# A two-layer transformer on one core: three places in a hand-written step order, and other buffer places

## What is computed

```python
x = _layernorm(x + _L0_attn_ref(x, ...))   # 16 heads of 16, relu weights, causal
x = _layernorm(x + _L0_ffn_ref(x, ...))    # Hadamard-rotated weights, 256 -> 1024 -> 256
x = _layernorm(x + _L1_attn_ref(x, ...))   # 32 query heads, 8 key/value heads of 64, window of 64, RoPE, softmax
x = _layernorm(x + _L1_ffn_ref(x, ...))    # silu(gate) * up, down, 256 -> 1024 -> 256

def _layernorm(x, axis=-1, eps=1e-05):
    m = jnp.mean(x, axis=axis, keepdims=True)
    v = jnp.var(x, axis=axis, keepdims=True)
    return (x - m) / jnp.sqrt(v + eps)

# second feed-forward
gate = jnp.einsum('bsd,hd->bsh', x, w_gate)
up = jnp.einsum('bsd,hd->bsh', x, w_up)
gated = jax.nn.silu(gate) * up
return jnp.einsum('bsh,dh->bsd', gated, w_down)
```

## Time and profile before

| | us |
|---|---|
| median of 3 runs | 527.74 (526.45 to 528.85) |
| the profiled execution | 527.04 |
| its span, first to last instruction | 524.4 |
| PE busy | 472.9 (90%) |
| DVE busy | 385.0 (73%) |
| ACT busy | 335.9 (64%) |
| POOL busy | 236.1 (45%) |

### The profile page before, as it was taken

The page is one execution under the profiler, slowest core; times in us unless marked ns, Lnnn a source line. Parts: engine busy times, 40 slices in busy tenths (PEclk is TensorE's granted clock), DMA queues, the critical chain, the costliest instruction groups (busy, mean ns, idle before and its releaser), DMA issues.

```text
span 524.4 us, 10779 instructions
## 1 busy us (share of the span) xinstructions
PE 472.9 (90%) x3848; PEld 400.3 (76%) x3848; DVE 385.0 (73%) x675; ACT 335.9 (64%) x940; POOL 236.1 (45%) x167
## 2 busy tenths in 40 slices
PE   2899997999999975999999999988996988899994
PEld 2454654788889964899999999978896877788884
DVE  4455597778562689998898998889889974543534
ACT  3555555634643439888888989859888798332230
POOL 0377537221640756655566566545656523400001
PEclk9999998999999997999999999989999899999998
DMA  8500010033310000000000000001001222000101
GB/s 272 176 16 2 2 41 0 1 120 92 97 66 20 1 1 0 23 20 3 22 23 21 21 23 21 8 15 40 24 12 50 62 62 81 1 0 1 41 0 40
DMA packets 8611, 19.96 MB, mean 38 GB/s; under 512 B 1392, under 2 KB 2928, under 8 KB 8432
## 3 DMA queue, kind: packets, MB, share of 16 engines
q1 hardware_dynamic: 8560, 19.29, 11.9%
HBM read 18.23 MB, written 1.05 MB: 37 GB/s over the span
## 4 chain that ended last, share of the span: by engine, by line
PE 72%; DVE 11%; ACT 8%; issue 5%; POOL 1%; DMA 1%; DVEq 0%; POOLq 0%; ACTq 0%; SPq 0%
PE psum L383 16%; PE psum L385 15%; PE psum L384 15%; PE psum L614 5%; PE psum L430 4%; PE psum L602 4%; PE psum L592 4%; ACT probs L846 4%; PE psum L448 4%; PE psum L573 2%; DVE minus_max L1122 1%; PE psum L582 1%; DVE rope_cos_part L1078 1%; DMA raw_chunks<-in_w 1%; DVE out_t_low L897 1%
## 5 line engine op out<-in xcount | busy, mean ns | idle before, releaser
L846 ACT ACTIVATE probs<-psum,minus_max 128x128 f32<-128x128 f32 x256 | 92.6, 398 | 18.7 <-PE psum L592 10.4
L1240 POOL TENSOR_TENSOR rope_sin_part<-qkv_rows,sin_weighted 128x640 f32<-128x640 f32 x32 | 49.1, 1556 | 62.3 <-DVE rope_cos_part L1091 39.5
L1249 POOL TENSOR_TENSOR rms_inverse<-rms_inverse,minus_half 128x20 f32<-128x20 f32 x16 | 64.0, 3999 | 1.3
L846 ACT ACTIVATION_READ_ACCUMULATOR probs<-psum,minus_max 128x1 f32 x256 | 60.4, 236 | 0.0
L818 ACT CAST hidden_high<-hidden 128x512 fp32r<-128x512 f32 x32 | 19.8, 620 | 62.4 <-DVE hidden L1037 62.4
L1122 DVE TENSOR_REDUCE minus_max<-psum 128x4 f32<-128x512 f32 x64 | 42.4, 684 | 15.7 <-PE psum L592 14.3
L383 PE MATMUL psum<-x_t_high,ug_high 128*128 128x512 f32 x128 | 51.2, 400 | 0.0
L385 PE MATMUL psum<-x_t_high,ug_low 128*128 128x512 f32 x128 | 50.7, 396 | 0.0
L384 PE MATMUL psum<-x_t_low,ug_high 128*128 128x512 f32 x128 | 50.4, 394 | 0.0
L1116 DVE TENSOR_TENSOR probs<-probs,prob_inverse 128x512 f32<-128x512 f32 x64 | 47.6, 744 | 2.2
L383 PE MATMUL psum<-qkv_high,x_t_high 128*128 128x384 f32 x128 | 46.3, 362 | 0.0
(11 more groups left out here) (146 smaller groups left out, 1403.4 us busy)
## 6 DMA issues: line engine op xcount, KB each, us to landing
raw_chunks<-in_ug SPq DMA_DIRECT2D x8, 512.0 KB, 3.9
raw_chunks<-in_wout SPq DMA_DIRECT2D x16, 256.0 KB, 2.8
raw_chunks<-in_qkv SPq DMA_DIRECT2D x8, 384.0 KB, 3.3
raw_chunks<-in_x SPq DMA_DIRECT2D x2, 512.0 KB, 4.5
raw_chunks<-in_w SPq DMA_DIRECT2D x2, 512.0 KB, 6.4
down_tree<-in_down SPq DMA_DIRECT2D x1, 1024.0 KB, 8.4
x_rows<-in_x_rows SPq DMA_DIRECT2D x2, 512.0 KB, 4.8
raw_chunks<-in_down SPq DMA_DIRECT2D x2, 512.0 KB, 3.4
```

Source lines behind the costliest of these rows:

```text
L846: e = nc.scalar.activation(pr[:, c, q, :], o[:, q * P:(q + 1) * P], ACT.Exp, bias=negm[:, c, q:q + 1], accum_out=psum1[:, c, q:q + 1])
L1240: last = nc.gpsimd.tensor_tensor(ov[:, :, :, z, :], rv[:, :, :, 1 - z, :], sv[:, :, :, z, :], ALU.mult)
L1249: nc.gpsimd.tensor_tensor(r, r, half[:], ALU.pow).then_inc(rr_done, 1)
```

## The change

Every step of a feed-forward is cut in two, `up(layer, n)` and `down(layer, n, *halves)`, and the layer norm in `ln_add`, `ln_stats`, `ln_norm` and POOL's `ln_half`. `later_steps` is replaced by tables for each engine: `..._FILL` (from the feed-forward's tile 10 to the seventh pass), passes 7 to 12 by the old pass tables, `..._DRAIN` (the rest of the passes and the first 8 tiles of the second feed-forward), and a short list for the end. Within a pass nothing is put in another order. What each engine does is otherwise in the old order, with these exceptions:

1. In the fill, DVE does `ln(1, 1)` before `values1(1)`, `rope_sums(0)`, `square_sums(1)`, `normed(0)` and `cosines(1)`, not after them; POOL's part stands before `sines(1)`. `xt(2, 1)` comes earlier: on PE after the first q transpose of iteration 0 rather than of iteration 1, on ACT before `squares(2)`, on DVE right after `cosines(1)`.
2. At the start of the second feed-forward PE does `up 1 3` before `down 1 0`, `down 1 1` and `xt(3, 1)`; DVE does `up 1 2` before `ln(2, 1)`, and `up 1 3` before its part of `xt(3, 1)`; ACT does `up 1 3` before its part.
3. In the last tiles the downs follow three ups behind, and the downs 13, 14 and 15 of the last batch run first for the first half of its rows and then for the second. DVE's additions and statistics follow each half, as before.
4. The weight pieces of the second feed-forward are split in the order ug 0, ug 1, down 0, ug 2, ug 3, down 1 (before: four ug, two down).

The buffers lie elsewhere: the weights of both feed-forwards and `qkv` with high and low side by side for each piece, `wout_low` behind `k_t`, and six slots instead of three for the hidden tiles of the second feed-forward. The waits follow the new neighbours. An extract:

```diff
-FLAG = 2
+HIDDEN_SLOTS = [3, 6]
-FFN1_CHUNKS = [("ug1", c) for c in range(4)] + [("down1", c) for c in range(2)]
+FFN1_CHUNKS = [("ug1", 0), ("ug1", 1), ("down1", 0), ("ug1", 2), ("ug1", 3), ("down1", 1)]
...
+VECTOR_FILL = [("up", 0, 10), ("up", 0, 11), ("xt", 2, 0), ("up", 0, 12), ("up", 0, 13), ("up", 0, 14), ("up", 0, 15),
+    ("values1", 0), ("square_sums", 0), ("cosines", 0), ("ln_add", 1, 1, 0), ("ln_stats", 1, 1, 0),
+    ("ln_add", 1, 1, 1), ("ln_stats", 1, 1, 1), ("ln_norm", 1, 1, 0), ("ln_norm", 1, 1, 1), ("values1", 1),
...
+def last_steps():
+    s = []
+    for n in range(8, B * NI):
+        s.append(("up", 1, n))
+        if n != 12:
+            s.append(("down", 1, n - 2 if n < 12 else n - 3))
+        if n == NI + 1:
             s.append(("ln", 3, 0))
-    s.append(("ln_last",))
+    for half_ in range(2):
+        s += [("down", 1, n, half_) for n in range(B * NI - 3, B * NI)]
+        s += [("ln_add", 3, 1, half_), ("ln_stats", 3, 1, half_), ("ln_half", half_)]
+    s += [("ln_norm", 3, 1, half_) for half_ in range(2)]
...
             qn = place(s, "roped", [TT, GN], F32)
+            qt1 = place(s, "q_t", [2, NQ, 2, WIN], F32)
+            place(s, "until_down0", [512])
+            kt1 = place(s, "k_t", [2, T], F32)
             wol = place(s, "wout_low", [2, 2, C], F32R)
-            qt1 = place(s, "q_t", [2, NQ, 2, WIN], F32)
-            kt1 = place(s, "k_t", [2, T], F32)
             pr = place(s, "probs", [4, 4, P], F32)
...
+            def down(layer, n, *halves):
...
+                for t in [2 * half_ + t2 for half_ in halves or range(2) for t2 in range(2)]:
...
             def up(layer, n):
+                if layer and n == 0:
+                    for read in (ss_done, cos_done, sin_done, v1_done, rope_sum):
+                        act.wait_ge(read, NIT)
...
             def turn1k(k):
+                if k == 0:
+                    filled(act, ("ffn", 0, NI + 6, 1))
...
             def exps(k, c):
                 if k:
                     filled(act, ("turn1p", k - 1, c))
+                else:
+                    filled(act, ("ffn", 0, B * NI - 1, 0))
...
             def normed(k):
                 if k == 0:
-                    filled(dve, ("y", 1, B - 1, 1))
+                    filled(dve, ("ffn", 0, NI + 3, 0))
```

More of the change, by code:

```diff
@@ new lines @@
+GPSIMD_DRAIN = [("sines", 11), ("wout", 8), ("rms_inverses", 11), ("ln", 2, 0), ("sines", 12), ("wout", 9),
+    ("rms_inverses", 12), ("sines", 13), ("wout", 10), ("rms_inverses", 13), ("sines", 14), ("wout", 11),
+    ("rms_inverses", 14), ("chunk", ("ug1", 0)), ("sines", 15), ("wout", 12), ("rms_inverses", 15),
+    ("chunk", ("ug1", 1)), ("wout", 13), ("chunk", ("down1", 0)), ("wout", 14), ("chunk", ("ug1", 2)), ("wout", 15),
+    ("chunk", ("ug1", 3)), ("chunk", ("down1", 1)), ("ln", 2, 1)]
@@ L360, in post_ln_two_layers, with up_weights, down_weights @@
         hi_no = {}
+        def up_weights(layer, c, z):
+            return ug0[c // 2][:, z, c % 2, :] if layer == 0 else w1["ug1", c][:, z, :]
+        def down_weights(layer, c, z):
+            return dn0[c][:, z, :] if layer == 0 else w1["down1", c][:, z, :]
         block = ctx.enter_context(nc.Block())
@@ L387, in _, with first @@
             acc = {}
+            begun = set()
+            def first(step, k):
+                new = (step, k) not in begun
+                begun.add((step, k))
+                return new
             def x_ready(layer, b):
@@ new lines, in up @@
+            def up(layer, n):
+                b, i = divmod(n, NI)
+                if i == 0:
+                    x_ready(1 + 2 * layer, b)
+                if layer == 0:
+                    emptied(pe, *[("prep_ug", i // 2, m) for m in range(KB)])
+                else:
+                    chunk_wait(pe, ("ug1", i // 2))
+                wh, wl = [up_weights(layer, i // 2, z) for z in range(2)]
+                for u in (1, 0):
+                    o, done = claim(("ffn", layer, n, u))
+                    for kb in range(KB):
+                        at = kb * 512 + (i % 2) * 256 + u * P
+                        mm = three(o, (wh[:, at:at + P], wl[:, at:at + P]), (xh[:, b, kb, :], xl[:, b, kb, :]),
+                                   kb == 0, kb == KB - 1)
+                    mm.then_inc(done, 1)
@@ L685, in chunk_target @@
                 return [a[:, c % 2].rearrange("p k t -> p (k t)") for a in (woh, wol)]
-            return [a[:, c, :] for a in {"qkv": (qkvh, qkvl), "ug1": (ug1h, ug1l), "down1": (dn1h, dn1l)}[name]]
+            return [(qkv[:, c] if name == "qkv" else w1[name, c])[:, z, :] for z in range(2)]
         @block.sync
```

309 lines of the change are left out of this document (169 added, 140 removed), and 42 rows, old and new, of tables (SCALAR_DRAIN, SCALAR_FILL, SCALAR_FIRST, TENSOR_DRAIN).

## The result

The changed kernel took 531.30 us, the median of 4 runs (530.36 to 532.65); the kernel before, beside it on the same chip, 527.10 (526.25 to 528.85, 4 runs). The ratio is 1.0074, with a 95% interval of 1.0042 to 1.0106: slower by about 4 us. The forecast was 532.5, with a range of 528.6 to 535.2. The profiled execution took 531.57 with a span of 529.9, against 527.04 and 524.4: 5.5 us longer.

The account below looks back on a forecast made before the run. PE was taken to bound the attention passes, DVE the fill (182 to 212 us). Fill 2.7, second feed-forward 1.4 plus clock 1.7, end -1.0 made +4.8: 532.5 us, own range 530.5 to 534.5, 8 in 10 528.6 to 535.2.

Parts of the forecast that it names:

- What costs nothing: Whole kernel: buffer places, added waits, chunk order and cut steps cost nothing; `normed(0)`'s dropped wait frees nothing.
- Place 1, the mechanism: Fill, 178 to 212 us: early `ln(1,1)` waits 1.97, starts 180.28; `normed(0)` ends 193.5; PE waits 8.4, then about 1.5.
- Place 1, the term: Fill: `maxima(1,0)` starts at 214.7 against 212.01, +2.7 that stays; bounds +0.65 and +4.45.
- so `scores1(0,0)` is done about 201.3: Fill: after half-clock PE work and ACT's copies ending about 200.1, scores end about 201.3 and `maxima(0,0)` starts at 201.35.
- The payback: Fill, after `normed(1)`: early `xt(2,1)` saves DVE 1.28, its wait falls from 0.72 to about 0.25; +4.45 becomes +2.7.
- In the fill I expect one such stretch again, so nothing is added there: Fill: one half-clock stretch as before, so no clock cost is added to the forecast there.
- Place 2, the idle: Second feed-forward's start: `ln(2,1)` starts at 456.87, 5.66 later; PE arrives 4.24 later; idle 1.32 becomes 2.74, +1.4.
- Place 2, the clock: Second feed-forward's start: the 2.74 idle drops the clock to half for some 3.4 us, +1.7.
- The rival with full clock there, 530.8: Second feed-forward's start: clock holds, as an idle between 2.31 and 2.53 or below decides; 530.8, chance 0.20.
- Place 3: Kernel's end: last three downs by halves; DVE's second addition starts 0.32 after PE's last matmul starts, 517.10 for 518.06, -1.0.
- The sum: Whole kernel: 2.7 + 1.4 + 1.7 - 1.0 = +4.8 on a span of 524.4, 532.5; chance 0.48.
- The shared pair: Fill: by the skill's GpSimd/VectorE rule `cosines(1)` waits for the POOL power and ends 3.6 later; +0.8, 533.3, chance 0.03.

Follow-up runs that it names:

- best_fill_free: Changed kernel with the fill's old order and DVE's `ln(2,1)` again before `up 1 2`, plus 24 unread matmuls into a free bank in PE's 6.08 us wait: 525.54 us, 0.9959.
- stall_filled: Changed kernel plus 32 unread 512-column matmuls in PE's list ahead of its wait for `normed(0)` (8.58 us): ratio 1.0036 to the kernel before.

## Why the prediction was right, and where not

- **What costs nothing**: right. With the three places undone the ratio was 0.9991 (0.9977 to 1.0005).
- **Place 1, the mechanism**: right, step by step. `ln(1,1)` started at 180.28 + 0.77, to the hundredth (after 1.90 of idle, 1.97 forecast), and `normed(0)` ended at 194.50 where I had 193.5 + 0.77. The waits of 8.58 and 0.95 answer to the forecast 8.4 and 1.5.
- **Place 1, the term**: mis-sized, 4.3 in this trace (3.6 to 3.8 in others with the same fill) for my 2.7; 1.84 of it is there without the half clock. Of the 1.6 that are missing, 0.2 is `normed(0)`. The step that failed is "so `scores1(0,0)` is done about 201.3": by the trace it took 9.04 from `roped` to the first maxima, and I had 7.85 (1.2). I had let the half clock last about as long as behind the 6.09, some 3.4 us, and it lasted 5.7. By the four traces with this fill (8.32 with 4.1 us of it, 9.04 with 5.7) that is most of the difference. From there to `normed(1)`'s end it took 4.42 where I had 4.95 (-0.5), for the sine products no longer ran beside that step. The payback was 1.1 and not 1.75 (+0.7): DVE's wait ahead of `maxima(1,0)` grew to 0.85, where I had let it shrink to 0.25. "In the fill I expect one such stretch again, so nothing is added there" was the thought behind it, and it is wrong. The stretch moved from a place where it is free, behind the 6.09 (shown by best_fill_free), to one where it lies on DVE's path and costs 1.8 to 2.5, by how long it lasts (shown by stall_filled).
- **Place 2, the idle**: right. With the 4.96 by which the last `pv1` is late taken off, `ln(2,1)` started at 456.86 for 456.87. The idle was 2.50 in all for 2.74, and the net 1.4 for 1.4. It came in two pieces, because I had not followed whose banks `down 1 0` takes.
- **Place 2, the clock**: wrong, +1.7 that didn't come; the full clock there is one of the signs of being wrong that I had named. The rival with full clock there, 530.8, described the trace. Its reason, that an idle between 2.31 and 2.53 decides, was wrong too: at the two later idles 2.33 lost the clock and 2.62 kept it. That the two pieces of 1.65 and 0.85 kept the clock is a reading; whether one piece of 2.5 would have lost it wasn't tried.
- **Place 3**: right, -0.97 for -1.0.
- **The sum**: 2.7 + 1.4 + 1.7 - 1.0 was 4.8; it was 4.3 + 1.4 + 0 - 1.0 = 4.7, and 0.77 of offset beside it. Two errors of 1.6 and 1.7 cancelled. The nearness of 532.5 to 531.3 is partly luck.
- **The shared pair**: no test. `cosines(1)` started at 194.53 and the power of iteration 1 at 194.65, so it never had to wait for it; it took its usual 1.49. But `cosines(2)`, at 210.70 in after, again took 1.49 while a power ran from 206.97 to 211.35. In the kernel with the fill undone `rope_sums(0)` again ran 1.49 inside a power of 3.53, as in the earlier trace rows.

## What to carry to other kernels

A work item that an engine does early because it is ready isn't free if the item's input ends last on that engine: here the layer norm, put ahead of steps that had their input already, made DVE wait 1.9 us, and put 6.3 us of layer norm (1.55 of them a wait for POOL) ahead of what PE waited for. A stretch of half clock has no price of its own; ask for each place who waits for PE there, since a dip cost 0 behind the 6.08 and at the first of the later idles, 1.1 to 1.2 at the second, and 1.8 to 2.5 us behind the 8.58. When steps are moved past each other, follow the buffers that they take and leave (here two PSUM banks) as well as their inputs.
